# Even and odd features side by side in one matmul, a conv loop with quantiser steps between its taps, and four buffers of block scales

## What is computed

```python
# level 0, conditional layer: h has 512 features
h = gelu(einsum('bnd,hd->bnh', x, fc1_w) + fc1_b)
shared = einsum('bnh,sh->bns', h, fc2_w) + fc2_b            # 96 outputs
expert_x = einsum('bnh,bph->bnp', h, experts_w[indices])    # 32 outputs, one of 16 experts a sequence
y = concatenate([shared, expert_x], -1)
# level 0, feed-forward
h = bit_linear(y, w1)                  # activations rounded to 127 steps of the row's maximum, weights to -1, 0, 1
h = silu(depthwise_conv1d(h, conv_w, conv_b))               # three taps along the tokens
x = x + bit_linear(h, w2)
# level 3, feed-forward: every operand rounded to 4-bit values with a scale for each 16 elements
hidden = silu(nvfp4(x, gate_w)) * nvfp4(x, up_w)
x = x + nvfp4(hidden, down_w)
```

## Time and profile before

| | us |
|---|---|
| median of three runs | 6531.6 |
| the profiled execution: its time | 6524.69 |
| the profiled execution: its span, first to last instruction | 6522.8 |
| mean granted TensorE clock, as a share of full speed | 0.927 |
| PE / DVE / ACT / POOL busy | 5572.6 / 3874.4 / 3391.1 / 3094.2 |

### The profile page before, as it was taken

One profiled execution on the slowest core, in us unless ns is written; L12 is line 12 of the kernel. 1 busy time (PEld: TensorE's weight loads), 2 busy tenths in 40 slices (PEclk: granted clock), 3 DMA queues, 4 the chain that ended last, 5 costly groups with the idle time before them and its releaser, 6 DMA issues. The chain is left out here.

```text
span 6522.8 us, 147859 instructions
## 1 busy us (share of the span) xinstructions
PE 5572.6 (85%) x52030; PEld 3487.7 (53%) x52030; DVE 3874.4 (59%) x6789; ACT 3391.1 (52%) x9840; POOL 3094.2 (47%) x1441
## 2 busy tenths in 40 slices
PE   5994777449986899999999999999999999997842
PEld 1333777324434566566656665666566556654531
DVE  2110000353331788588858876887788688866875
ACT  0000000231110799489949985997699679943431
POOL 0000000010001888488848875886688578841035
PEclk9999999858885999999999999999999999997965
DMA  7666777200000000000000000000000000000000
GB/s 203 180 156 126 84 84 83 36 22 6 10 2 15 10 0 0 18 1 0 0 18 1 0 0 18 0 0 14 5 0 0 14 5 0 0 14 14 6 4 10
DMA packets 260468, 188.94 MB, mean 29 GB/s; under 512 B 183598, under 2 KB 244174, under 8 KB 253366
## 3 DMA queue, kind: packets, MB, share of 16 engines
q1 hardware_dynamic: 198617, 118.59, 10.1%
q10 hardware_dynamic: 61453, 64.76, 4.1%
HBM read 127.21 MB, written 56.08 MB: 28 GB/s over the span
## 5 line engine op out<-in xcount | busy, mean ns | idle before, releaser
L1567 POOL TENSOR_TENSOR rs<-ss,minus_half 128x16 f32<-128x16 f32 x386 | 1127.4, 2921 | 278.7 <-DVE ss L1644 277.9
L1485 ACT ACTIVATE s_ps<-s_ps,low 128x128 f32<-128x128 f32 x3072 | 1050.0, 343 | 81.6 <-DVE low L1655 76.3
L1565 POOL TENSOR_TENSOR t<-t 128x1024 f32<-128x1024 f32 x386 | 909.4, 2356 | 152.6 <-DVE t L1633 151.9
L1572 POOL TENSOR_TENSOR qk<-t,rs 128x1024 f32<-128x1024 f32 x386 | 734.2, 1902 | 63.7 <-POOL rs L1567 23.7
L1485 ACT ACTIVATION_READ_ACCUMULATOR s_ps<-s_ps,low 128x1 f32 x3072 | 641.7, 209 | 0.0
L1655 DVE TENSOR_REDUCE low<-s_ps 128x4 f32<-128x512 f32 x768 | 494.5, 685 | 203.9 <-PE s_ps L1313 203.9
L488 POOL MEMSET pad<- 128x1040 f32 x1 | 1.0, 964 | 1204.7 <-SPq L478 1204.7
L1627 DVE TENSOR_TENSOR t<-qk_ps,rot 128x1024 f32<-128x1024 f32 x386 | 472.4, 1224 | 162.4 <-PE qk_ps L1279 148.5
L1664 DVE TENSOR_TENSOR p<-s_ps,rec 128x512 f32<-128x512 f32 x768 | 530.7, 691 | 30.5
L253 PE MATMUL h_ps<-h_x,h_w 9*128 9x512 bf16 x4096 | 440.8, 629 | 78.1 <-DMA h_w<-rows_w1s 62.9
L1319 PEld LDWEIGHTS pT_ps<-ident,p 128*128 128x128 f32 x3072 | 354.7, 141 | 267.4 <-issue 265.1
(11 more groups left out here) (359 smaller groups left out, 9698.0 us busy)
## 6 DMA issues: line engine op xcount, KB each, us to landing
h_x<-rows_xs SPq DMA_DIRECT2D x512, 72.0 KB
rows_hs<-h_parts ACTq DMA_DIRECT2D x88, 384.0 KB, 7.1
z_fm<-rows_hs SPq DMA_DIRECT2D x256, 72.0 KB
x_fm<-rows_hs SPq DMA_DIRECT2D x256, 72.0 KB
wqkv<-in_wqkv SPq DMA_DIRECT2D x7, 1536.0 KB, 6.5
o_w<-rows_exs ACTq DMA_DIRECT2D x512, 18.0 KB
rows_xs<-z_fm ACTq DMA_DIRECT2D x12, 384.0 KB, 5.6
rows_exs<-s_exp ACTq DMA_DIRECT2D x9, 512.0 KB, 8.6
```

Source lines behind the costliest of these rows:

```text
L1485: ins = act.activation(s_ps[:, e, i * P:(i + 1) * P], s_ps[:, e, i * P:(i + 1) * P], ACT.Exp, bias=low[:, c % 2, e, i:i + 1], scale=-1.0, ...
L1565: pool.tensor_tensor(t1[:, i, :], t1[:, i, :], t2[:, i, :], ALU.add).then_inc(s_["t12"], 1)
L1567: pool.tensor_tensor(rs[:, i, :], ss[:, i, :], R.minus_half[:, 0:2 * UH], ALU.pow).then_inc(s_["rs"], 1)
L1572: pool.tensor_tensor(qk[:, i, :].rearrange("p (h d) -> p h d", d=DH), t1[:, i, :].rearrange("p (h d) -> p h d", d=DH), rs[:, i, :].unsquee ...
```

## The change

**Front.** The features are ordered even ones first, then odd ones (in `layout`, on the host: `two`). `rows_hs` has 18 rows for 256 pairs of features, rows 0 to 8 for the even one of a pair and 9 to 17 for the odd one. In `level0_out` a chunk is 32 pairs: 4 DMAs of SP with 18 rows each (twice the bytes, half as many DMAs, runs of 256 bytes as before), 8 of ACT for the expert's weights (as large as before, and as many in all), and 128 matmuls of 18 x 128 against 18 x 256, 8192 in all in place of 16384. The moving operand has the even feature's weights in rows 0 to 8 and in the first of two interleaved halves of columns, the odd one's in rows 9 to 17 and the other half, and zeros elsewhere. So `o_w` is cleared first: four memsets on POOL and four on DVE, of 4096 fp32 each; SP waits for the first pair before the first of the shared weights and for all before its loads of `h`, ACT waits for all before the other weights. `load_w` is 32 DMAs in place of 16, each half as large. PSUM then holds the even and the odd sums apart, and DVE joins them in three steps for each sequence in place of one. In `split` the two copies to bf16 read the upper half of each fp32 word in place of the word, a cut in place of a rounding.

```diff
-    t(0, eng.tensor_copy(parts(2), src))
+    t(0, eng.tensor_copy(parts(2), high(src)))
...
-        w = m.sb("o_w", [P, 4, HID, EO], BF16)
+        w = m.sb("o_w", [P, 4, 2, PAIRS, EO], BF16)
...
             def _(pool):
                 m.credit(pool)
+                for i in range(4):
+                    clear(pool, i, 2)
...
+                for i in range(4):
+                    sp.wait_ge(zeroed[i], at(1))
+                    if i == 0:
+                        load_w(sp, 0)
...
+                for i in range(4):
+                    act.wait_ge(zeroed[i], at(1))
                 for i in range(1, 4):
                     load_w(act, i)
...
-                                mm = pe.matmul(ps[c][b][:, 0:P], chunk(i % 4)[rows(b), t, :],
-                                               w[rows(b), :, i * TC + t, :], start=i + t == 0, stop=False,
-                                               skip_group_check=True)
+                                mm = pe.matmul(ps[c][b][:, 0:2 * P], chunk(i % 4)[rows(b), t, :],
+                                               w[rows(b), :, :, i * TC + t, :].rearrange("p a e o -> p (a e) o"),
+                                               start=i + t == 0, stop=False, skip_group_check=True)
```

```diff
-                pipeline(dve, NG, 1, [(residual, 3), (scale2, 2), (conv_taps, 1), (quant1, 0)])
+                pipeline(dve, NG, 2, [(residual, 3), (scale(0), 2), (scale(1), 2), (deq(0), 1), (deq(1), 1), (tap(0), 1),
+                                      (scale(2), 2), (deq(2), 1), (tap(1), 1), (scale(3), 2), (deq(3), 1), (tap(2), 1),
+                                      (tap(3), 1), (quant1, 0)])
...
-                pipeline(pe, NG, 1, [(turn3, 3), (turn2, 2), (hidden, 1), (turn1, 0)])
+                pipeline(pe, NG, 2, [(turn3, 3), (to_tokens(0), 2), (to_tokens(1), 2), (hidden(0), 1), (hidden(1), 1),
+                                     (to_features(0), 2), (to_tokens(2), 2), (hidden(2), 1), (down(0), 2),
+                                     (to_features(1), 2), (to_tokens(3), 2), (hidden(3), 1), (down(1), 2),
+                                     (to_features(2), 2), (down(2), 2), (to_features(3), 2), (down(3), 2),
+                                     (turn1, 0)])
```

```diff
-        hb8 = m.sb("hb8", [P, 2, NBH])
+        hb8 = m.sb("hb8", [P, 4, NBH])
...
-                    dve.wait_ge(s_["hq"], at(k - 2))
+                    dve.wait_ge(s_["hq"], at(k - 4))
```

More of the change, by code:

```diff
@@ L141, in t, with high @@
         eng.wait_ge(step, at(base + x))
-    t(0, eng.tensor_copy(parts(2), src))
+    def high(a):
+        v = a.bitcast(BF16)
+        return bass.AP(v.tensor, v.offset + 1, [v.ap[0]] + [[2 * s, n] for s, n in a.ap[1:]])
+    t(0, eng.tensor_copy(parts(2), high(src)))
     t(1, eng.tensor_tensor(rest, src, parts(2), ALU.subtract))
-    t(2, eng.tensor_copy(parts(1), rest))
+    t(2, eng.tensor_copy(parts(1), high(rest)))
     t(3, eng.tensor_tensor(parts(0), rest, parts(1), ALU.subtract))
@@ L345, in level0_out, with rows @@
         xback = m.dma_sem("o_xback")
-        used, y_out = (m.sem(f"o_{n}") for n in ("used", "y_out"))
-        def rows(b):
-            return slice(32 * b, 32 * b + ROWS)
+        zeroed = [m.sem(f"o_zeroed{i}") for i in range(4)]
+        used, even_, both_, y_out = (m.sem(f"o_{n}") for n in ("used", "even", "both", "y_out"))
+        def rows(b, e=None):
+            return slice(32 * b, 32 * b + 2 * ROWS) if e is None else slice(32 * b + e * ROWS, 32 * b + e * ROWS + ROWS)
         def chunk(cc):
@@ L418, in _ @@
             def _(dve):
+                for i in range(4):
+                    clear(dve, i, 0)
                 def join(k, j, c):
@@ L627, in residual, with scale, deq, tap @@
                     dve.tensor_tensor(x, x, ot_ps[:, :], ALU.add).then_inc(s_["x"], 1)
-                pipeline(dve, NG, 1, [(residual, 3), (scale2, 2), (conv_taps, 1), (quant1, 0)])
+                def scale(b):
+                    return lambda k, j, c: scale2(k, b)
+                def deq(t):
+                    return lambda k, j, c: dequant(k, t)
+                def tap(t):
+                    return lambda k, j, c: taps(k, t)
+                pipeline(dve, NG, 2, [(residual, 3), (scale(0), 2), (scale(1), 2), (deq(0), 1), (deq(1), 1), (tap(0), 1),
+                                      (scale(2), 2), (deq(2), 1), (tap(1), 1), (scale(3), 2), (deq(3), 1), (tap(2), 1),
+                                      (tap(3), 1), (quant1, 0)])
             @block.scalar
@@ L655, in silu, with big, f @@
                                        bias=0.0, scale=conv[:, t, 0:1]).then_inc(s_["tap0"], 1)
-                        if t > 0:
-                            one(t - 1)
-                    one(HT - 1)
-                def round2(k, j, c):
-                    for b in range(GB):
+                    return f
+                def big(b):
+                    def f(k, j, c):
                         n = k * GB + b
@@ L696, in turn1, with hidden, f @@
                               start=True, stop=True).then_inc(s_["bcast"], 1)
-                def hidden(k, j, c):
-                    pe.wait_ge(s_["q1c"], at(k))
-                    for t in range(HT):
+                def hidden(t):
+                    def f(k, j, c):
+                        if t == 0:
+                            pe.wait_ge(s_["q1c"], at(k))
                         pe.wait_ge(s_["deq"], at(k * HT + t - 2))
@@ L724, in to_features, with down, f @@
                         mm.then_inc(s_["q2T"], 1)
-                    def down(b):
+                    return f
+                def down(b):
+                    def f(k, j, c):
                         n = k * GB + b
@@ L735, in down @@
                         mm.then_inc(s_["o"], 1)
-                    to_tokens(0)
-                    to_tokens(1)
-                    for b in range(GB):
-                        to_features(b)
-                        if b + 2 < GB:
-                            to_tokens(b + 2)
-                        down(b)
+                    return f
                 def turn3(k, j, c):
```

175 lines of the change are left out of this document (100 added, 75 removed).

## The result

| | us |
|---|---|
| changed kernel, median of 4 (6319.31 to 6335.16) | 6327.59 |
| kernel before, median of 4 beside it | 6536.01 |
| ratio, with its 95% interval | 0.9675 (0.9654 to 0.9696) |
| profiled execution of the changed kernel: time, span | 6319.31, 6317.2 |

The account below looks back on a forecast made before the run. Loads of `h` were taken to bind `level0_out`. From the profiled 6524.7 us, -133 (stage) +4 (lead) +1 (copies) +3 (join) -38 and -22 (feed-forwards) gave 6339.7; with 6.9 to the median, 6347, range 6276 to 6490.

Parts of the forecast that it names:

- The bound: `level0_out`: loads of `h` bind, nine engines never resting at 35.0 ns a packet, 257 packets a microsecond, 591 us.
- the 437 us of PE: `level0_out`: matmul price goes by columns, 53.3 ns for 256 columns, 6.83 us a chunk, 437 us for 64 chunks.
- Rival A: `level0_out`: the price belongs to the packet, load rate stays 257 a microsecond, stage 583 us, total 6488 us; chance 0.20.
- Rival C: `level0_out`: PE cheaper than by columns, some 40 ns a matmul, DMAs bind, total 6324 us; chance 0.07.
- Stage: `level0_out` matmuls: 437 us of PE plus 4% for sharing engines with expert and code loads, 455 us, gain 133.
- Rival B: `level0_out`: rows collide, load rate 231 packets a microsecond, stage 648 us, total 6553 us; chance 0.04.
- Lead: `level0_out` before the matmuls: clearing costs 17 us, faster weight loads give back 13, net +4 us (-5 to +33).
- Copies and join: Copies reading upper halves cost +1 us; three join steps for each sequence in place of one cost +3 us.
- First feed-forward: `level0_ffn`: waits for `h_ps` and later `st_ps` go, two taps shut out, slot 23.1 us, gain 38 us (25 to 50).
- Last feed-forward: `level3_ffn`: DVE's maximum starts right behind `hid`, one small step shut out, 1.54 us saved 14 times, gain 22 us.
- The signs: Profile: 8192 matmuls 53 ns apart, queue over 320 packets a microsecond, lead 60 to 70 us, `level0_ffn` slot 22 to 24.
- Rival D: Both feed-forwards: the new orders bring nothing, total 6407 us; chance 0.09.

Follow-up runs that it names:

- the nine-row loads: Changed kernel with each 18-row load of `h` issued as two nine-row loads: `level0_out` matmuls 448.3 us, or 335.6 us with half the matmul columns.
- the kernels with one part each: Kernel before with only the first stages, only the first feed-forward or only the last feed-forward changed: ratios 0.9761, 0.9952 and 0.9963.
- The kernel with rows apart: Kernel before with the nine rows of each group on every third partition, zeros between, 25-row matmuls: `level0_out` matmuls 567.9 us.

## Why the prediction was right, and where its terms were off

**The bound: right time, wrong cause.** The forecast names the loads of `h` as what bounds `level0_out`, nine engines that never rest at 35 ns a packet. That step failed. A share of 9/16 is no limit (the nine-row loads show it without binding), the loads had landed 3.2 us before PE needed them, and PE's idle time went, for 97.5 of some 126 us, on stalls inside chunks, where it waits for its program. The evidence stood in the earlier trace rows: `[3.21 <-issue]`. The forecast calls what stands between the bursts "the breaks between them", says that half as many matmuls save only these, and then leaves them to the loads. They were the gain: 126 us of idle time became 8.4, and PE's busy time fell by another 24.6, from 462.3 to 437.6. The time came out because the sum needs no more than that the old bound goes away and PE's own 437 us are left. That it did go away was luck as far as this reasoning reaches; the 437 us of PE were reasoned out, and right. Whether the loads had a share in it after all, by slowing the program's packets, stays open.

**Rival A.** It falls on the rate alone: 326 packets a microsecond in the same number of packets, not 257. But so does the forecast's reason against it. That packets cost 23 and 42 ns in two stretches is no sign of crowded rows, since a packet also takes longer where less is asked of the queue. The Trainium skill (SBUF — State Buffer, "Door 1: The DMA port swizzle") has a point that I passed over: a partition and the one 32 above it are on the same port, so the four groups of rows crowd in pairs. No run here separates that. The picture of two engines rather than four on the same rows of one load is not borne out: two nine-row loads did as well as one of eighteen.

**PE.** Forecast 53.3 ns for 256 columns, measured 53.4. Rival C is out: the price goes by columns.

**Stage.** Forecast 455 us, measured 446. The 4% for expert rows and code was too much: the loads had far more room (452 packets a microsecond) than the 361 of the earlier trace rows, which was a short stretch and no ceiling, and the breaks at the loop's jumps back cost 8.3 us only. Rival B is out too: it needed 231 packets a microsecond.

**Lead.** The largest miss: +4 forecast, -12 measured. I charged the clearing with 17 us because SP and ACT wait. The memsets take 16 us, but SP waits for the first quarter alone before its weights; 4.3 us show, and the rest lies beside its loads. The weights then took 588.5 - 541.7 = 46.8 us for 63.1, a gain of 16 where I had 13.

**Copies and join.** +4 forecast, -3.0 in `level0_hidden` and the tail together. The twelve join steps take 4.0 us where four took 0.9, and the tail grew by 0.4: something else in it ends last. The 3.4 us of `level0_hidden` are nothing to explain, since in these executions it lasted 529 to 552 us, and both ends come from kernels with the same code there.

**First feed-forward.** 38 forecast, 33.9 measured. Where the slot comes from was right term for term: 4 us of waits behind the residual stay (3.9, all of it for `ot_ps`), those for `h_ps` go, and POOL's step shuts out taps. I had two taps shut out by 0.85, 1.7 us; four were, three beside line 542 and one beside line 533, by 0.66 to 0.84 each, 3.0 us. So 23.8 for 23.1. Stretched taps were named among the signs of a wrong forecast, though the sum itself priced two of them; four stretched, and the slot still came within 0.7 us.

**Last feed-forward.** 22 forecast, 26.3 measured. I expected one small step shut out, two were; I also expected the first to slip through the opening, and it was the second. The period still came to 12.6, not 13.0: lines 2334 and 2335 end with POOL's step, where I had them start behind it, and that is 0.4 us more than the 1.54.

**The signs.** Matmuls (8192, 53.4 ns, 446 us), queue (326 a microsecond) and `level0_ffn`'s slot (23.4 to 23.9 us) came as forecast; the lead, at 51.1 for 60 to 70, did not. A queue at over 320 was no sign for the forecast's cause: it follows from PE's pace, whatever bound before.

**The sum.** By the stages the change is worth 218 us where I had 185; other stages' scatter of +12.4 in that one execution hides part of it, and the medians differ by 208. Rival D is out by the kernels with one part each.

## What to carry to other kernels

Before calling a queue the bound because its share is full, look at where the consumer stalls. If it stalls at places where the program has no wait, look when its instructions arrive, and try fewer, larger matmuls before faster loads. Taking columns away shows only that the columns don't bind; it leaves the loads and the delivery of the program both as suspects. And keep small DVE steps that lie beside POOL's long ones off the shared port: one PSUM bank for three tiles of 64 columns gave 28.6 us of the stage, more than the reordering it corrects.

## What the runs showed of the hardware

- A stream of small matmuls can run short of its own program. With 9x128 or 9x64 matmuls in bursts of 128, PE stalled where nothing is waited for, and all 180 such stalls in two kernels ended 1.2 to 2.0 us after a 16 KB packet on the `instruction` queue. 256-column matmuls, at 53.4 ns each, had no such stall inside a chunk.
- Four row tiles of few rows move 4.3 (64 columns a matmul) to 4.8 (512) columns a nanosecond. The kernel with rows apart had a granted clock of 0.50 in this stretch, which is the lower of its two levels (1.2 GHz), after 25-row matmuls in place of 9-row ones:

```profile
750.00:780.00 30.00, 24.80 (x904) 23.33 (x899) 0.00 (x0) 0.00 (x0) 0.00 (x0) 0.50 0.39 90
```

  Its bursts of 128 matmuls take 3.60 us there, as at 1.00, 2.4 GHz, in the kernel before: in these two traces the clock makes no difference to them.
- A DMA of ACT to nine partitions three apart takes 0.76 us to issue, one to nine neighbours 0.29.
- A memset of 4096 fp32 elements on DVE has a row of 3.47 us, but four in a row start 4.27 us apart.
- A DVE step of 64 elements from SBUF to SBUF takes 0.20 us alone and up to 1.99 beside POOL; with PSUM on one side such steps take 0.23 to 0.29 beside POOL.
